# Two-layer decoder, attention of layers 0 and 1: SyncE issues a step's shift rows ahead of the loads of QK

## Chip, cores and metric

One core of one Trainium2 chip runs the whole program. The metric is the device time of one execution in microseconds (us), the median of several executions.

## What is computed

A decoder of two layers on x (32 batches, 128 tokens, width 128). Each layer is self attention, cross attention with a context, and a mixture of experts, each behind a layer norm and added to x:

```python
x = x + _L0_attn_ref(_layernorm(x), ...)            # 16 heads of width 8, 4 KV heads repeated
x = x + _L0_xattn_ref(_layernorm(x), ctx_1024, ...) # 16 heads of width 8
x = x + _L0_ffn_ref(_layernorm(x), ...)             # 8 experts, top 2, plus a shared one
x = x + _L1_attn_ref(_layernorm(x), ...)            # 4 averaged heads of width 64, relative bias
x = x + _L1_xattn_ref(_layernorm(x), ctx_1024, ctx_1024, mask, ...) # 16 heads of width 8, masked
x = x + _L1_ffn_ref(_layernorm(x), ...)             # 8 experts, top 2, plus a shared one
```

The three attentions with heads of width 8 go through the function `head_attention`: once for the two of layer 0 (tiles named `heads_...`, 64 batches in all), once for the cross attention of layer 1 (tiles named `cross_...`, 32 batches). For a batch and a head it is softmax(q k^T * scale) v.

## The kernel before, in words

`head_attention` is a software pipeline that each of the five instruction queues writes out by itself, step by step (`steps`, with one step per batch, a group being two batches). At step k:

- TensorE (`scores`) computes the scores of batch k+3 for their row maxima (`ps_max`, L973) and the transposed scores of batch k for the exponents (`ps_exp`, L977), in two parts v = 0 and 1; between them it turns the maxima of batch k+2 (L1045), and it projects q (even k) and k (odd k) of group k//2+5 (L1016, L1026).
- VectorE reduces the maxima (L776) and writes the shift of a batch as two bf16 numbers a head (L804). ScalarE copies the turned shift into `shiftT` (L870), takes the exponents (L847), and copies the projections out (L886, L890).
- GpSimd splits q and k of a group into three bf16 parts each (L690 to L693) and stores them to DRAM as `qk_parts` (L697, 384 KB a group).
- SyncE brings them back in the layout that the score products want: the tile `QK[p]` (four of them, one a group, used in turn) holds for each half of the heads 48 rows of parts and two rows for the shift. At an even step k it loads half 0 of group k//2+3, at the next step half 1 (L619, three DMAs of 192, 128 and 64 KB). At every step it places the two shift rows of batch k+2 (L629, two DMAs of 4 KB).

The shift rows of a batch go into the extra rows of the QK tile, so the exponent product of batch k yields scores minus maximum. It needs them when step k starts (`shift_placed`, waited for in `scores` at v = 0), two steps after they were issued. The first product of the maxima of group g is in step 2g-3 and needs both halves of the group's QK (`qk_placed`).

What SyncE waits for: before half 0, the store of that group (`qk_stored`, a semaphore that GpSimd's DMA raises) and the exponent scores of the batch before (`exp_scored`), since the tile is used again; before half 1, nothing of its own; before the shift rows, ScalarE's copy (`shiftT_ready`). SyncE works strictly in the order in which its program lists these, so whatever stands behind a wait waits too. In steps 22 to 50 of the `heads` part, and in the `cross` part, an even step also loads 128 KB of the context (`kvT`, L638), last in the step. All of SyncE's DMAs use one hardware queue.

The lines around the change are the function `emit` inside `sp_program`; who waits for them is in `scores`:

```python
if v == 0:
    pe.wait_ge(qk_placed[q_of], t.turn(96, 1, MA))
...
if v == 0:
    pe.wait_ge(shift_placed[t.k % 2], t.group(32, 32))
```

The loops that are rolled (`LOOPS`: steps 4 to 19 and 36 to 51 in the `heads` part, 4 to 11 in the `cross` part) use the same `emit`.

Of the kernel before, what the change touches and what calls it, by code (L numbers as in the profile page):

```python
# [24 lines left out]
B, S, D = 32, 128, 128  # L25
H, HD = 16, 8
G = 2
NG = B // G
GT = G * S
RING = 4  # L30
# [4 lines left out]
ROWS = sum(hi - lo for lo, hi in WINDOWS) * HD  # L35
HALVES = 2
HH = H // HALVES
BASE = 64
TILE, SLOT = 32, 16
SHIFT = 2  # L40
FA, SA, LA, MA, VA = 5, 4, 3, 3, 3
# [37 lines left out]
def need(engine, semaphore, value):  # L79

    if isinstance(value, int) and value <= 0:
        return
    engine.wait_ge(semaphore, value)


def apart(engine, t, turns):


    if t.reg is not None:
        engine.sem_inc(turns, 1)  # L90
# [313 lines left out]
def head_attention(nc, sem, name, x_sb, norm, ident, identb, QK, layers, mask, scale, prepare, opening, make_lead, staging, make_follow, handed):  # L404
# [14 lines left out]
    with ExitStack() as ctx:  # L419
        tiles = ExitStack()  # L420

        def sb(label, shape, dt=F32):
            return tiles.enter_context(nc.sbuf_tensor(f"{name}_{label}", shape, dt))
# [13 lines left out]
        NB_ALL, NG_ALL = NL * B, NL * NG  # L437
# [12 lines left out]
        shiftT = [sb(f"shiftT{p}", [SHIFT * H, S], BF16) for p in range(2)]  # L450
# [21 lines left out]
        turns_sp, turns_pool, turns_dve = sem("turns_sp"), sem("turns_pool"), sem("turns_dve")  # L472
# [23 lines left out]
        shiftT_ready = sem("shiftT_ready")  # L496
        shift_placed = [sem(f"shift_placed{p}") for p in range(2)]
# [39 lines left out]
        def slot(t, ahead=0):  # L537

            return (t.k // G + ahead) % RING

        def layer_of(t, group):

            return min((t.k // G + group) // NG, NL - 1)
# [29 lines left out]
        def load_qk_weights(engine, i):  # L573
            w = layers[i][0]
            for dst, src in ((wq, w["q"]), (wk, w["k"]), (bq, w["bq"]), (bk, w["bk"])):
                engine.dma_start(dst[i][:], src).then_inc(qk_loaded[i], 16)

        def load_vo_weights(engine, i):
            w = layers[i][0]
            for dst, src in ((wv, w["v"]), (wo, w["o"]), (bv, w["bv"]), (bo, w["bo"])):  # L580
                engine.dma_start(dst[i][:], src).then_inc(loaded[i], 16)

        def sp_program(sp):
            if kv_src[0] is not None:
                sp.dma_start(kvT[0][:], kv_src[0][:, 0:GT]).then_inc(kv_loaded[0], 16)
            if opening is not None:
                for i in range(len(Opening.PIECES) - 1):
                    opening.load_x(sp, i)
                opening.place_ones(sp, QK)
            for i in range(0 if opening is None else 1, NL):  # L590
                load_qk_weights(sp, i)
                load_vo_weights(sp, i)
            if opening is not None:
                opening.load_table(sp)
            if masked:
                sp.dma_start(mask_in[:, 0, :], mask[0]).then_inc(loaded[0], 16)
                for r in range(2):
                    sp.dma_start(mask_in[r * BASE:(r + 1) * BASE, 1, :], mask[1][(1 - r) * BASE:(2 - r) * BASE, :]).then_inc(loaded[0], 16)
            if lead is not None:
                prepare.load(sp, 0, 1, prepare.early(), prep_early)  # L600

            follow.sp_start(sp)

            def emit(t):
                if t.has(-2 * LA, 2 * NG_ALL - 1 - 2 * LA):

                    p, half = slot(t, LA), t.k % 2
                    if half == 0:
                        if opening is not None and t.k == -2 * LA:
                            sp.wait_ge(opening.ones_placed, 16 * HALVES * RING)  # L610
                        sp.wait_ge(qk_stored[p % 2], t.pair(16, LA, 1))
                        apart(sp, t, turns_sp)
                        need(sp, exp_scored, t.batch(PAIRS))
                        apart(sp, t, turns_sp)
                    row = 0
                    for lo, hi in WINDOWS:
                        n = (hi - lo) * HD
                        source = bass.AP(qk_dram[p], half * HH * GT, [[H * GT, n], [(PARTS + lo) * D * GT, 2], [1, HH * GT]])
                        sp.dma_start(QK[p][half * BASE + row:half * BASE + row + n].rearrange("r c h t -> r c (h t)"), source).then_inc(qk_placed[p], 16)  # L619
                        row += n  # L620
                if t.has(1 - MA, NB_ALL - MA):

                    p, j = (t.k + MA - 1) // G % RING, (t.k + MA - 1) % G
                    turned = shiftT[(t.k + MA - 1) % 2]
                    sp.wait_ge(shiftT_ready, t.batch(1, MA))
                    apart(sp, t, turns_sp)
                    for i in range(SHIFT):
                        at = ROWS + i
                        sp.dma_start(QK[p][at:at + BASE + 1:BASE, 0, :, j * S:j * S + S], turned[i:SHIFT * H:SHIFT, :]).then_inc(shift_placed[(t.k + MA - 1) % 2], 16)  # L629
                to = layer_of(t, FA + 1)  # L630
                if kv_src[to] is not None and t.k % 2 == 0 and t.has(-2 * FA, 2 * NG_ALL - 4 - 2 * FA):

                    p = slot(t, FA + 1)
                    need(sp, v_made, t.group(1, FA + 2 - RING))
                    apart(sp, t, turns_sp)
                    need(sp, qk_made, t.group(1, FA + 2 - RING))
                    apart(sp, t, turns_sp)
                    sp.dma_start(kvT[p][:], kv_src[to][:, bass.ds(t.group(GT, (FA + 1 - to * NG) * GT), GT)]).then_inc(kv_loaded[p], 16)  # L638
                if t.reg is None and prepare.splits and t.k in LATE_LOAD:
                    if t.k == LATE_LOAD[0]:  # L640
                        sp.wait_ge(prep_lo, Prepare.PIECES)
                    prepare.load(sp, LATE_LOAD.index(t.k), len(LATE_LOAD), prepare.late(), prep_late)
                if prepare.by_rel is not None and t.k == LAST:
                    prepare.load_bias(sp, by_rel_stored, bias_loaded)
                if t.reg is None and 0 <= t.k - CLEAR < CLEARS and follow.sp_clear is not None:
                    follow.sp_clear(sp, t.k - CLEAR)
                if t.reg is None and t.k == NB_ALL - 2 and follow.sp_tables is not None:
                    follow.sp_tables(sp)
            steps(sp, emit, FIRST, LOOPS, LAST)
            follow.sp(sp)  # L650

# [2142 lines left out]
```

## Time and profile before

| | |
|---|---|
| median of 3 executions | 1070.99 us (1059.96 to 1075.71) |
| the profiled execution | 1062.24 us, of it span 1060.1 us |
| granted TensorE clock, mean | 0.966 |
| PE / DVE / ACT / POOL busy | 917.9 / 823.2 / 664.8 / 648.1 us |
| `heads` part (scores on TensorE) | from 31 to about 355 us |
| `cross` part | from 726 to about 907 us |

PE is TensorE, DVE VectorE, ACT ScalarE, POOL GpSimd, SP SyncE; a q behind the name is the queue that issues (SPq, POOLq). In a row of the timeline the first number is the start in us, the second the duration; in brackets stands how long the engine was idle before and what ended it. A wait row reads: who waited, for whom, us in total, times, longest.

### The profile page before, as it was taken

To read this page: it belongs to the slowest core of one execution; us is meant where nothing else is said; L and a number is where in the kernel's file an instruction comes from. 1 tells how busy PE (TensorE), PEld (TensorE's weight loads), DVE (VectorE), ACT (ScalarE), POOL (GpSimd) and SP (SyncE) were. 2 spreads that over 40 slices of the span, in tenths; PEclk is the share of its full clock that TensorE was granted. 3 is DMA by queue.
4 is the path that set the end of the run, shared out by engine and by line. 5 is a ranking of instruction groups with operands and counts; after the bars stand their busy time and mean duration, and the time that the engine had idled before them with its cause. 6 is when DMAs were issued, how large, how long until landed. Compare 5 with 4: busy or idle time off the path is not lost.

```text
span 1060.1 us, 33068 instructions
## 1 busy us (share of the span) xinstructions
PE 917.9 (87%) x10494; PEld 673.0 (63%) x10494; DVE 823.2 (78%) x2110; ACT 664.8 (63%) x1609; POOL 648.1 (61%) x1020
## 2 busy tenths in 40 slices
PE   3599878889988789999998889977999998778997
PEld 1366656656665577777777677755566555556885
DVE  6389888878988778888897888766788766757675
ACT  1177777768776633555665888763666666556775
POOL 7857787887785467720585787158767842333443
PEclk9999999989998879999999999999999999889999
DMA  5776667886675201232332101125555650054551
GB/s 146 164 178 135 123 144 165 175 176 139 148 186 146 75 38 63 92 99 77 104 107 64 37 28 29 42 46 132 136 121 138 142 109 4 18 200 160 199 198 30
DMA packets 81455, 119.65 MB, mean 113 GB/s; under 512 B 16720, under 2 KB 62704, under 8 KB 80288
## 3 DMA queue, kind: packets, MB, share of 16 engines
q1 hardware_dynamic: 66704, 85.24, 32.6%
q0 software_dynamic: 9472, 27.27, 8.9%
q10 hardware_dynamic: 5136, 5.31, 2.3%
q8 instruction: 80, 1.31, 0.6%
q14 instruction: 63, 0.52, 0.2%
HBM read 80.75 MB, written 36.18 MB: 110 GB/s over the span
## 4 chain that ended last, share of the span: by engine, by line
PE 50%; DVE 19%; issue 9%; POOL 9%; DMA 7%; ACT 4%; SPq 1%; POOLq 1%; DVEq 0%; ACTq 0%
DVE heads_neg_max L776 4%; PE experts_ps_gu L2502 4%; PE cross_ps_max L963 3%; DVE cross_neg_max L776 3%; DMA QK<-heads_shiftT 3%; PE experts_ps_gu L2504 2%; PE experts_ps_gu L2503 2%; PE cross_ps_max L973 2%; DMA heads_qk_parts<-heads_parts 2%; PE cross_ps_pv L995 2%; PE heads_ps_max L973 2%; PE experts_ps_y L2523 2%; PE heads_ps_pv L995 2%; PE experts_ps_y L2524 2%; POOL heads_rest L691 2%
## 5 line engine op out<-in xcount | busy, mean ns | idle before, releaser
L776 DVE TENSOR_REDUCE heads_neg_max<-heads_ps_max 128x8 f32<-128x1024 f32 x128 | 156.4, 1222 | 50.2 <-PE heads_ps_max L973 48.3
L847 ACT ACTIVATE heads_E<-heads_ps_exp 128x1024 f32<-128x1024 f32 x128 | 131.1, 1024 | 71.5 <-PE heads_ps_exp L977 69.9
L973 PE MATMUL heads_ps_max<-QK 48*128 48x128 bf16 x1024 | 83.4, 227 | 37.5 <-DMA QK<-heads_shiftT 17.7
L776 DVE TENSOR_REDUCE cross_neg_max<-cross_ps_max 128x8 f32<-128x1024 f32 x64 | 78.4, 1225 | 36.7 <-PE cross_ps_max L973 36.5
L2196 POOL DMA_INDIRECT experts_gathered<-experts_y_dram,experts_index x64 | 62.1, 971 | 69.1 <-DMA experts_y_dram<-experts_y_sb 49.2
L973 PEld LDWEIGHTS heads_ps_max<-QK 48*128 48x128 bf16 x1024 | 60.6, 98 | 67.8 <-issue 29.3
L847 ACT ACTIVATE cross_E<-cross_ps_exp 128x1024 f32<-128x1024 f32 x64 | 65.6, 1025 | 57.3 <-PE cross_ps_exp L977 57.3
L2418 ACT ACTIVATE experts_act_out<-experts_ps_gu 128x256 f32<-128x256 f32 x110 | 42.4, 385 | 81.8 <-PE experts_ps_gu L2504 80.6
L995 PE MATMUL heads_ps_pv<-heads_E,heads_V 128*32 128x128 f32 x2048 | 85.9, 287 | 0.5 <-issue 0.5
L1627 POOL TENSOR_TENSOR experts_hidden_lo<-experts_hidden,experts_hidden_hi 128x512 fp32r<-128x512 f32 x32 | 41.4, 1295 | 70.6 <-ACT experts_hidden_hi L1851 67.3
L977 PE MATMUL heads_ps_exp<-QK 50*128 50x128 bf16 x1024 | 80.8, 223 | 0.7 <-ACT heads_E L847 0.6
L2172 POOL DMA_INDIRECT experts_xs_dram<-QK,experts_index x64 | 61.5, 962 | 28.0 <-DMA experts_xs_dram<-QK,experts_index 20.2
L2523 PE MATMUL experts_ps_y<-experts_down,experts_hT_hi 128*128 (+1 forms) x220 | 67.8, 329 | 6.6 <-DVE experts_hT_lo L2322 4.4
L995 PEld LDWEIGHTS heads_ps_pv<-heads_E,heads_V 128*32 128x32 f32 x2048 | 49.9, 112 | 28.2 <-issue 20.7
L2317 DVE TENSOR_TENSOR experts_hidden<-experts_act_out,experts_ps_gu 128x256 f32<-128x256 f32 x110 | 46.2, 420 | 25.7 <-ACT experts_act_out L2418 19.7
L1765 DVE TENSOR_TENSOR experts_hidden<-experts_ps_gate,experts_share 128x512 f32<-128x512 f32 x64 | 43.7, 688 | 24.0 <-ACT experts_ps_gate L1845 15.5
L977 PEld LDWEIGHTS heads_ps_exp<-QK 50*128 50x128 bf16 x1024 | 58.1, 97 | 1.5 <-ACT heads_E L847 1.0
L2524 PE MATMUL experts_ps_y<-experts_down,experts_hT_lo 128*128 (+1 forms) x220 | 58.1, 285 | 0.0
L1851 ACT CAST experts_hidden_hi<-experts_hidden 128x512 fp32r<-128x512 f32 x72 | 44.3, 615 | 20.8 <-DVE experts_hidden L1765 14.9
L1266 ACT ACTIVATE shared_E<-shared_scores,shared_neg_max 128x128 f32<-128x128 f32 x128 | 49.8, 393 | 6.7 <-DVE shared_probs L1215 6.7
L296 POOL TENSOR_TENSOR norm_var_eps<-norm_moments,norm_eps 128x2 f32<-128x2 f32 x64 | 12.6, 197 | 67.5 <-DVE norm_moments L289 57.1
L963 PE MATMUL cross_ps_max<-cross_drop_q,identb 64*64 64x512 bf16 x256 | 39.8, 387 | 10.2 <-DVE cross_neg_max L776 9.8
(323 smaller groups left out, 3134.3 us busy)
## 6 DMA issues: line engine op xcount, KB each, us to landing
experts_share<-experts_cT_dram SPq DMA_DIRECT2D x7, 2304.0 KB, 8.7
heads_qk_parts<-heads_parts POOLq DMA_DIRECT2D x32, 384.0 KB, 5.8
QK<-heads_qk_parts SPq DMA_DIRECT2D x64, 192.0 KB
QK<-heads_qk_parts SPq DMA_DIRECT2D x64, 128.0 KB
cross_qk_parts<-cross_parts POOLq DMA_DIRECT2D x16, 384.0 KB, 3.9
QK<-cross_qk_parts SPq DMA_DIRECT2D x32, 192.0 KB
experts_xs_dram<-load_stats SPq DMA_DIRECT2D x26, 192.0 KB, 2.8
experts_xs<-experts_xs_dram SPq DMA_DIRECT2D x78, 64.0 KB
```

Of the source, the lines that this page charges most:

```text
L776: nc.vector.tensor_reduce(neg_max[(t.k + MA) % 2][:, :, heads_of(v)], ps_max[:].rearrange("q a (h k) -> q a h k", h=HU), AX.X, ALU.max, ne ...
L847: nc.scalar.activation(E[:, :, heads_of(v), :], ps_exp[:].rearrange("k a (h q) -> k a h q", h=HU), ACT.Exp, scale=scale).then_inc(exp_done, 1)
L963: nc.tensor.matmul(ps_max[here, half, :].rearrange("q (h k) -> q h k", h=HU), identb[here, here], drop_q[here].unsqueeze(1).to_broadcast([ ...
L973: last_max = nc.tensor.matmul(ps_max[:, half, i * S:(i + 1) * S], QK[q_of][rows, 0, h, max_of], QK[q_of][rows, 1, h, max_of], start=not ma ...
L977: last_exp = nc.tensor.matmul(ps_exp[:, 1 - half, i * S:(i + 1) * S], QK[e_of][rows, 1, h, exp_of], QK[e_of][rows, 0, h, exp_of], start=no ...
L995: last = nc.tensor.matmul(ps_pv[TILE * i:TILE * (i + 1), v * S:(v + 1) * S], V[p][:, j, window:window + TILE], E[:, half, h, :], start=hal ...
L1266: last = nc.scalar.activation(E[:, s, :], scores[t.k % 2][:, s // 2, s % 2, :], ACT.Exp, bias=neg_max[t.k % 2][:, s:s + 1], accum_out=sums ...
L2172: pool.indirect_dma_start(xs_dram[h], bass.IndirectOffsetOnAxis(index[:, choice, b:b + 1], 0), xn[b // MG][:, b % MG, :], None).then_inc(s ...
L2196: pool.indirect_dma_start(gathered[n % GATHERS][:], None, y_dram[h], bass.IndirectOffsetOnAxis(index[:, choice, b:b + 1], 0)).then_inc(loa ...
L2317: nc.vector.tensor_tensor(hidden[u % 3][:], act_out[u % 3][:], ps_gu[:, u % 2, F:], ALU.mult).then_inc(hidden_ready, 1)
L2523: nc.tensor.matmul(out, hT_hi[u % 3][:, these], both, start=c == 0, stop=False, skip_group_check=True)
L2524: last = nc.tensor.matmul(out, hT_lo[u % 3][:, these], both, start=False, stop=c == 1, skip_group_check=True)
```

## The change

In `emit` of SyncE's program the block with the shift rows stands ahead of the block that loads QK, where it stood behind it. Waits, sizes, semaphores and the number of DMAs are the same.

```diff
             def emit(t):
+                if t.has(1 - MA, NB_ALL - MA):
+
+                    p, j = (t.k + MA - 1) // G % RING, (t.k + MA - 1) % G
+                    turned = shiftT[(t.k + MA - 1) % 2]
+                    sp.wait_ge(shiftT_ready, t.batch(1, MA))
+                    apart(sp, t, turns_sp)
+                    for i in range(SHIFT):
+                        at = ROWS + i
+                        sp.dma_start(QK[p][at:at + BASE + 1:BASE, 0, :, j * S:j * S + S], turned[i:SHIFT * H:SHIFT, :]).then_inc(shift_placed[(t.k + MA - 1) % 2], 16)
                 if t.has(-2 * LA, 2 * NG_ALL - 1 - 2 * LA):
...
-                if t.has(1 - MA, NB_ALL - MA):
-
...
```

Lines L605 to L613 are now the shift rows (their DMA is L613), and the loads' DMA is L628; before they were L629 and L619. The kernel's other lines keep their numbers.

SyncE's queue at the start of the `heads` part, before the change: the rows from half 0 of the third group on (`heads_qk_parts` are the stored parts, `heads_shiftT` the shift).

```order
L619 DMA QK<-heads_qk_parts 24x2x2048 [waits heads0_qk_stored0]
L619 DMA QK<-heads_qk_parts 16x2x2048
L619 DMA QK<-heads_qk_parts 8x2x2048
L629 DMA QK<-heads_shiftT 2x8x128 [waits heads0_shiftT_ready]
L629 DMA QK<-heads_shiftT 2x8x128
L619 DMA QK<-heads_qk_parts 24x2x2048
L619 DMA QK<-heads_qk_parts 16x2x2048
L619 DMA QK<-heads_qk_parts 8x2x2048
```

And after it, the same place:

```order
L613 DMA QK<-heads_shiftT 2x8x128 [waits heads0_shiftT_ready]
L613 DMA QK<-heads_shiftT 2x8x128
L628 DMA QK<-heads_qk_parts 24x2x2048 [waits heads0_qk_stored0]
L628 DMA QK<-heads_qk_parts 16x2x2048
L628 DMA QK<-heads_qk_parts 8x2x2048
L613 DMA QK<-heads_shiftT 2x8x128 [waits heads0_shiftT_ready]
L613 DMA QK<-heads_shiftT 2x8x128
L628 DMA QK<-heads_qk_parts 24x2x2048
```

The first batch's shift rows no longer stand behind the wait for the store of the third group, and half 1 of that group now stands behind the shift rows of the second batch.

In the rolled loop before the change, an even step and the odd step after it (QK1 is the group's tile, QK3 the one that gets the shift):

```order
L619 DMA QK1<-heads0_qk_parts1 24x2x2048 [waits heads0_exp_scored]
L619 DMA QK1<-heads0_qk_parts1 16x2x2048
L619 DMA QK1<-heads0_qk_parts1 8x2x2048
L625 ISA
L629 DMA QK3<-heads0_shiftT0 2x8x128 [waits heads0_shiftT_ready]
L629 DMA QK3<-heads0_shiftT0 2x8x128
L619 DMA QK1<-heads0_qk_parts1 24x2x2048
L619 DMA QK1<-heads0_qk_parts1 16x2x2048
L619 DMA QK1<-heads0_qk_parts1 8x2x2048
L625 REGISTER_ALU
L629 DMA QK3<-heads0_shiftT1 2x8x128 [waits heads0_shiftT_ready]
L629 DMA QK3<-heads0_shiftT1 2x8x128
```

After it:

```order
L613 DMA QK3<-heads0_shiftT0 2x8x128 [waits heads0_shiftT_ready]
L613 DMA QK3<-heads0_shiftT0 2x8x128
L620 ISA
L83 ISA [waits heads0_qk_stored1]
L628 DMA QK1<-heads0_qk_parts1 24x2x2048 [waits heads0_exp_scored]
L628 DMA QK1<-heads0_qk_parts1 16x2x2048
L628 DMA QK1<-heads0_qk_parts1 8x2x2048
L609 REGISTER_ALU
L613 DMA QK3<-heads0_shiftT1 2x8x128 [waits heads0_shiftT_ready]
L613 DMA QK3<-heads0_shiftT1 2x8x128
L628 DMA QK1<-heads0_qk_parts1 24x2x2048
L628 DMA QK1<-heads0_qk_parts1 16x2x2048
```

Half 1 stood right behind the even step's shift rows; now it stands behind the odd step's, which wait for ScalarE one step later. Half 0 stands behind the even step's.

## Rows read from the trace of the kernel before

**Rows 1.** The page, part 4: the chain that ended last, by line.

```profile
DVE heads_neg_max L776 4%; PE experts_ps_gu L2502 4%; PE cross_ps_max L963 3%; DVE cross_neg_max L776 3%; DMA QK<-heads_shiftT 3%; PE experts_ps_gu L2504 2%; PE experts_ps_gu L2503 2%; PE cross_ps_max L973 2%; DMA heads_qk_parts<-heads_parts 2%; PE cross_ps_pv L995 2%; PE heads_ps_max L973 2%; PE experts_ps_y L2523 2%; PE heads_ps_pv L995 2%; PE experts_ps_y L2524 2%; POOL heads_rest L691 2%
```

**Rows 2.** Waits of the whole span: us in total, times, longest.

```profile
PE heads_ps_max L973 <- DMA QK<-heads_shiftT: 17.7, 11, 6.3
...
PEld heads_ps_max L973 <- DMA QK<-heads_qk_parts: 5.1, 3, 2.8
```

**Rows 3.** Timeline of TensorE, first score products of steps -3, -1, 0.

```profile
30.85 0.35 PEld L973 LDWEIGHTS heads_ps_max<-QK 48*128 48x128 bf16 x8 [0.65 <-DMA QK<-heads_qk_parts]
...
41.92 0.62 PE L973 MATMUL heads_ps_max<-QK 48*128 48x128 bf16 x8 [2.11 <-DMA QK<-heads_qk_parts]
...
52.00 0.26 PE L973 MATMUL heads_ps_max<-QK 48*128 48x128 bf16 x1 [6.35 <-DMA QK<-heads_shiftT]
```

**Rows 4.** Timeline of SyncE's queue at the start of the heads part.

```profile
22.35 2.18 SPq L619 DMA_DIRECT2D QK<-heads_qk_parts  x6
...
45.18 1.32 SPq L629 DMA_DIRECT2D QK<-heads_shiftT  x2
...
47.82 1.07 SPq L629 DMA_DIRECT2D QK<-heads_shiftT  x2
```

**Rows 5.** Timeline of ScalarE: the copy of the first batch's shift.

```profile
37.49 0.26 ACT L870 COPY heads_shiftT<-heads_ps_qk 32x128 bf16<-32x128 bf16 x1 [0.18 <-PE heads_ps_qk L1045]
```

**Rows 6.** Timeline, first product of step 3 and of step 5 on TensorE.

```profile
66.27 0.23 PE L973 MATMUL heads_ps_max<-QK 48*128 48x128 bf16 x1
...
74.91 0.23 PE L973 MATMUL heads_ps_max<-QK 48*128 48x128 bf16 x1
```

**Rows 7.** SyncE's queue, half 1 of step 3, then shift rows of steps 3, 11.

```profile
65.68 1.42 SPq L619 DMA_DIRECT2D QK<-heads_qk_parts  x3
...
68.67 1.06 SPq L629 DMA_DIRECT2D QK<-heads_shiftT  x2
...
102.95 1.07 SPq L629 DMA_DIRECT2D QK<-heads_shiftT  x2
```

**Rows 8.** SyncE's queue: loads (L619), and the shift rows of steps 19, 25, 39, 53.

```profile
135.84 1.06 SPq L619 DMA_DIRECT2D QK<-heads_qk_parts  x3
...
139.71 1.16 SPq L629 DMA_DIRECT2D QK<-heads_shiftT  x2
...
171.44 1.06 SPq L629 DMA_DIRECT2D QK<-heads_shiftT  x2
...
208.84 1.26 SPq L619 DMA_DIRECT2D QK<-heads_qk_parts  x3
...
243.22 1.08 SPq L629 DMA_DIRECT2D QK<-heads_shiftT  x2
...
306.56 1.06 SPq L629 DMA_DIRECT2D QK<-heads_shiftT  x2
```

**Rows 9.** The chain in order of time: start us, us, the shift rows' transfer.

```profile
137.64 4.43 DMA QK<-heads_shiftT
...
211.83 6.59 DMA QK<-heads_shiftT
```

**Rows 10.** DMA issues in 78 to 97 us, 745 to 870 us: count, KB, us to landing.

```profile
heads_qk_parts<-heads_parts POOLq DMA_DIRECT2D x2, 384.0 KB, 4.8
...
cross_qk_parts<-cross_parts POOLq DMA_DIRECT2D x11, 384.0 KB, 3.6
```

**Rows 11.** Timeline of GpSimd: two stores of parts in a row.

```profile
110.61 0.91 POOL L697 DMA_DIRECT2D heads_qk_parts<-heads_parts  x1 [0.68 <-POOL heads_parts L693]
...
119.88 0.91 POOL L697 DMA_DIRECT2D heads_qk_parts<-heads_parts  x1 [0.75 <-POOL heads_parts L693]
```

**Rows 12.** Cross part: half 1 and shift rows of step 3, first product of step 5.

```profile
755.61 1.68 SPq L619 DMA_DIRECT2D QK<-cross_qk_parts  x3
...
759.25 1.06 SPq L629 DMA_DIRECT2D QK<-cross_shiftT  x2
...
767.27 0.23 PE L973 MATMUL cross_ps_max<-QK 48*128 48x128 bf16 x1
```

More of the change, by code:

```diff
@@ L620, in emit @@
                         row += n
-                if t.has(1 - MA, NB_ALL - MA):
[L623 to L629, printed above, removed]
                 to = layer_of(t, FA + 1)
```

## The prediction

> **What bounds the kernel now.** I read the page's chain first: it is spread thin, over TensorE, VectorE, GpSimd and DMA; what concerns this change is the 3% on the transfer of the shift rows and the 2% on the store of the parts [rows 1]. Outside the two stretches that run `head_attention` nothing is touched. The waits then say what stands against TensorE: 17.7 us for shift rows, 11 times, and 5.1 us for the parts [rows 2]. One of the 11 is 6.35 us before step 0; ahead of it, step -1 had waited 2.11 us for a load of QK [rows 3]. Why step 0 waited is seen on SyncE: ScalarE had the shift of batch 0 ready at 37.75 us [rows 5], its DMAs left only at 45.18 us [rows 4], since half 0 of the third group stood ahead and waited for GpSimd's store.
>
> The other ten (11.35 us) have the same shape in small. GpSimd stores a group every 9.27 us [rows 11]; the load of half 0 leaves when that store has landed, the shift rows behind it, and they travel behind its packets: issued at 137.09 us, after the load at 135.84, they land at 137.64 + 4.43 = 142.07 us [rows 8, 9]. They hold 8 KB, so nearly all of that is the load ahead of them.
>
> The pace is read from the issue times of the shift rows of odd steps, which follow TensorE's step by a fixed bit. A pair of steps (a group) took (102.95 - 68.67) / 4 = 8.57 us in steps 3 to 11, (139.71 - 102.95) / 4 = 9.19 in steps 11 to 19, (171.44 - 139.71) / 3 = 10.58 in 19 to 25, (243.22 - 171.44) / 7 = 10.25 in 25 to 39 (the stretch with the most other transfers), and (306.56 - 243.22) / 7 = 9.05 in 39 to 53 [rows 7, 8].
>
> **What is removed.** Shift rows no longer wait for a store or for half 0 of their own step. At the start they can leave at 37.8 us instead of 45.18, and step 0 can start about 4.2 us (half a pair) after step -1, at 46.1 instead of 52.00. Not all of the 5.9 us stays: step 1 needs group 2, whose half 0 still waits for the store that ends at about 44.1 us (half 0 left just ahead of the shift rows at 45.18) and whose half 1 follows at about 46.3. A pair of halves issued together was awaited for 30.85 - 22.35 = 8.5 us [rows 3, 4], so they are there at 52.6 to 55, and step 1, which began about 5.5 us after step 0, moves from 57.5 to 53 to 55. Bounds 0 and -5.9; I take -3 us.
>
> **What is added.** Both halves now leave later, and half 1 matters, for it is the last thing the next group needs. Take step 3: it starts at 66.27 us, half 1 left at 65.68, before the step even began; the shift rows of the step left at 68.67 [rows 6, 7]. After the change half 1 leaves behind them, 2.4 us (68.67 - 66.27) plus 1.1 us (two issues) into the step: at 69.8 us, 4.1 us later. Step 5, which needs it, started at 74.91 us. That leaves 5.1 us for a load that had 9.2. From then on the pair of steps can't be shorter than 2.4 + 1.1 + L = 3.5 + L, with L the time from issuing half 1 to its landing. The cover for the delay was the lead of the loads, and it is used up. Behind SyncE's new wait on ScalarE stand half 0, half 1 and the context loads; of these only half 1 has a reader within two steps (half 0 is issued a step earlier, and the context is read later).
>
> What is L? The trace gives the loads no landing, so it is bounded. From below by the nearest transfer of the same 384 KB, GpSimd's store, in 4.8 us in the heads part and 3.6 us in the cross part [rows 10]; the store reads 128 partitions where a load half writes 48, so I hold a load for hardly faster. From above by shift rows that travelled behind a load: load at 135.84, shift rows landed at 142.07, L at most 6.2 us in a quiet stretch; load at 208.84, shift rows landed at 211.83 + 6.59 = 218.42, at most 9.6 us in the dense one [rows 8, 9]. The pair in 8.5 us gives 4.3 us each as throughput, so one alone takes longer than that. I take 6.0 us in the quiet stretches, near the row of 6.2, and 8.0 us in the dense one, since the half before it will be a full step ahead instead of 2 to 3 us.
>
> A rule of the Trainium skill speaks for less: "DMA: Bandwidth & Descriptors", section "Anatomy of one DMA", fits a transfer by GpSimd's path as 2.0 us plus bytes / 436,000 per us, by which 393,216 bytes would need an estimated 2.9 us. By that rule L would fit into any pair and the loads' delay would cost nothing. The store, which is of just that kind, took 4.8 us here [rows 10], so the trace doesn't bear the fit out in this traffic; it counts for the rival with fast loads below.
>
> **The sum.** Quiet pair 3.5 + 6.0 = 9.5, dense pair 3.5 + 8.0 = 11.5:
> start -3; steps 3 to 11: 4 x (9.5 - 8.57) = +3.7; 11 to 19: 4 x (9.5 - 9.19) = +1.2; 19 to 25: 0 (L of 7 gives 10.5 against 10.58); 25 to 39: 7 x (11.5 - 10.25) = +8.8; 39 to 53: 7 x (9.5 - 9.05) = +3.2; two more pairs with loads after that, +1. Together +14.9, taken as +15 us. The 11.35 us of small waits for shift rows are inside these terms: they vanish, but the pair is then held by half 1, so they aren't subtracted again.
>
> In the cross part a pair takes 10.4 us, as TensorE itself is slower there. Half 1 would leave at 759.25 + 1.1 = 760.35 instead of 755.61, and is needed at 767.27: 6.9 us for a load, above the 6.2 [rows 12]. Term 0; TensorE's products hide it. If L were 8 there, it would cost 1.1 us in each of about 13 pairs.
>
> The profiled execution took 1062.24 us, so it would be 1077.2 us. The median of the three runs shown lies 8.75 us above the profiled one; I add half of that, about 4: 1081 us.
>
> **The rivals.**
> *Fast loads, faster.* If half 1 lands in 4.8 us, like the store, a quiet pair of 3.5 + 4.8 = 8.3 holds up nothing, and the waits for shift rows go. For it: the store's row, 17.7 us of waits removed. Against: the bound from the shift rows, and GpSimd's own 9.27 us a group, which would hold the middle stretches anyway. At its full 17.7 us: 1062.2 - 17.7 + 4 = 1049 us. It decides below an L of about 5.1 us.
> *GpSimd's pace hides it, no change.* With L at 5.6 a quiet pair is 9.1, about what it is now, as GpSimd stores every 9.27 us. Steps 3 to 11 cost 4 x 0.5 = +2, the start gives it back, and the dense pair with L at 6.7 is 10.2, as now. 1062.2 + 0 + 4 = 1066 us. For it: the middle stretches do look bound by GpSimd. Against: L must be well below both rows that bound it from above.
> *The dense stretch doesn't relax, much slower.* If L stays 9.6 us there, a pair is 13.1: 7 x 2.85 = +20 instead of +8.8; with 6.5 in the quiet pairs (+0.5 in 15 of them) the total is +34: 1062.2 + 34 + 4 = 1100 us. The cross part's +14 would belong to this case too. For it: the row of 9.6. Against: slower pairs thin the traffic out.
> That the change does not do what it says is excluded by the order of SyncE's queue.
>
> **How the numbers follow.** Forecast (+8 to +22) 0.40, no change (-5 to +8) 0.22, fast loads 0.12, much slower 0.26. Two per cent of the median is 21 us, about what a measurement can tell from no change. Faster by more: only the far end of fast loads, 0.03. Slower by more: 0.24 of the much slower case and 0.08 of the forecast, 0.32. The rest, 0.65, is within 2%. The range reaches down into fast loads, to 1054, and up past the much slower case to 1103; the forecast's own range is 1070 to 1092.
>
> **What would show it.** Right: the waits of TensorE for the shift rows fall from 17.7 us to under 3, and waits for `heads_qk_parts` rise from 5.1 to 20 us or more, all before odd steps; step 0 starts near 46 us; half 1 leaves 3.5 us into the odd step; pairs of 9.3 to 9.8 us in steps 3 to 19 and of 11 or more in 25 to 39; the cross part at 10.4 a pair with no wait for loads. Wrong: no waits for parts and pairs of 8.6 (L below 5.1), or GpSimd without a gap from step 5 to 20 and pairs of 9.2 with the waits elsewhere, or waits for parts in the cross part.

## The result, and the profile after

| | before | after |
|---|---|---|
| median (12 executions each) | 1060.56 us (1056.73 to 1075.71) | 1071.78 us (1068.27 to 1081.48) |
| ratio, 95% interval | | 1.0103 (1.0078 to 1.0128) |
| profiled execution, its span | 1062.24, 1060.1 us | 1070.25, 1068.2 us |
| granted TensorE clock, mean | 0.966 | 0.974 |

The change costs 1.0% (between 0.8 and 1.3%): slower, by less than the 2% that the forecast set as its mark. Between the medians it is 11.2 us, between the profiled executions 8.0: the one before lies 1.7 us above its median, the one after 1.5 below. The views below are of these two, so a few us of what they show can be theirs alone.

The chain that ended last, by line, in the page of after; it answers [rows 1]:

```profile
DMA QK<-heads_qk_parts 12%; PE experts_ps_gu L2502 4%; PE cross_ps_max L963 3%; DVE cross_neg_max L776 3%; SPq L613 3%; SPq L628 2%; PE experts_ps_gu L2504 2%; PE experts_ps_gu L2503 2%; PE cross_ps_max L973 2%; PE cross_ps_pv L995 2%; PE experts_ps_y L2523 2%; PE experts_ps_y L2524 2%; PE heads_ps_max L973 2%; PE experts_ps_hT L2510 2%; PE experts_ps_gate L1906 2%
```

The transfer of the shift rows (3% before) is gone from it, and the loads of QK, not among the lines listed before, head it with 12%, SyncE's issues (SPq) behind them. The waits say the same; they answer [rows 2]:

```profile
PE heads_ps_max L973 <- DMA QK<-heads_qk_parts: 36.2, 28, 4.6
POOL heads_parts L690 <- ACT heads_qk_full L890: 28.3, 19, 7.7
...
PEld heads_ps_max L973 <- DMA QK<-heads_qk_parts: 26.2, 15, 3.7
```

Waits for shift rows have left the list; those for the parts went from 7.2 us (5.1 of PEld [rows 2] and 2.1 of PE [rows 3]) to 62.4 us. PE and PEld are two views of TensorE that overlap, so this isn't 62 us of time. The middle row shows who waits in turn: GpSimd for ScalarE's copy of k (14.4 us before).

The timeline of TensorE, first score product of steps 0, 1, 3, 5, 7 and 17:

```profile
46.07 0.26 PE L973 MATMUL heads_ps_max<-QK 48*128 48x128 bf16 x1 [0.68 <-issue]
...
54.83 0.29 PE L973 MATMUL heads_ps_max<-QK 48*128 48x128 bf16 x1 [3.21 <-DMA QK<-heads_qk_parts]
...
65.31 0.23 PE L973 MATMUL heads_ps_max<-QK 48*128 48x128 bf16 x1
...
78.55 0.28 PE L973 MATMUL heads_ps_max<-QK 48*128 48x128 bf16 x1 [4.55 <-DMA QK<-heads_qk_parts]
...
89.57 0.23 PE L973 MATMUL heads_ps_max<-QK 48*128 48x128 bf16 x1
...
136.48 0.21 PE L973 MATMUL heads_ps_max<-QK 48*128 48x128 bf16 x1 [1.12 <-DMA QK<-heads_qk_parts]
```

SyncE's queue (now L613 the shift rows, L628 the loads): the start, then half 0 of step 2 (64.76), half 1 of steps 3, 15 and 31 (68.81, 130.49, 208.48), and the shift rows of steps 3, 11, 19, 25, 39 and 53:

```profile
37.30 1.12 SPq L613 DMA_DIRECT2D QK<-heads_shiftT  x2
...
45.99 1.20 SPq L628 DMA_DIRECT2D QK<-heads_qk_parts  x3
...
64.76 1.47 SPq L628 DMA_DIRECT2D QK<-heads_qk_parts  x3
67.70 1.06 SPq L613 DMA_DIRECT2D QK<-heads_shiftT  x2
68.81 1.46 SPq L628 DMA_DIRECT2D QK<-heads_qk_parts  x3
...
111.14 1.07 SPq L613 DMA_DIRECT2D QK<-heads_shiftT  x2
...
130.49 1.19 SPq L628 DMA_DIRECT2D QK<-heads_qk_parts  x3
...
148.18 1.07 SPq L613 DMA_DIRECT2D QK<-heads_shiftT  x2
...
176.64 1.07 SPq L613 DMA_DIRECT2D QK<-heads_shiftT  x2
...
208.48 1.28 SPq L628 DMA_DIRECT2D QK<-heads_qk_parts  x3
...
247.69 1.09 SPq L613 DMA_DIRECT2D QK<-heads_shiftT  x2
...
313.20 1.07 SPq L613 DMA_DIRECT2D QK<-heads_shiftT  x2
```

And the chain in order of time, which now gives the landing of half 1 (start plus duration; a row starts when the last of the three DMAs is issued):

```profile
46.87 7.92 DMA QK<-heads_qk_parts
...
69.94 8.29 DMA QK<-heads_qk_parts
...
131.36 4.89 DMA QK<-heads_qk_parts
...
209.44 6.54 DMA QK<-heads_qk_parts
```

Read them together: half 1 issued at 45.99 landed at 54.79, and step 1 began at 54.83; issued at 68.81 it landed at 78.23, step 5 began at 78.55; issued at 130.49 it landed at 136.25, step 17 began at 136.48. Step 3 began at 65.31 us, so its half 1 left 3.5 us into the step, and the pair up to step 5 took 13.2 us. Step 7 (89.57) had no wait for a transfer before it.

Where the 8 us came from, by the issue times of the shift rows of odd steps as for [rows 7, 8]:

| steps | a pair before | a pair after | change of the stretch |
|---|---|---|---|
| start, up to step 3 | | | 67.70 - 68.67 = -1.0 |
| 3 to 11 | 8.57 | 10.86 | +9.2 |
| 11 to 19 | 9.19 | 9.26 | +0.3 |
| 19 to 25 | 10.58 | 9.49 | -3.3 |
| 25 to 39 | 10.25 | 10.15 | -0.7 |
| 39 to 53 | 9.05 | 9.36 | +2.2 |
| sum at step 53 | | | 313.20 - 306.56 = +6.6 |

Issue times don't follow TensorE's step by a fixed bit everywhere: at step 25 before they came 3.75 us after its first product, at the table's other steps 2.4 to 2.7. By first products steps 19 to 25 and 25 to 39 change by -2.1 us each, instead of -3.3 and -0.7; their sum stays at -4. After step 53 the difference grows by 1.4 us more, 0.6 of it in the `cross` part.

The loss is not spread over the pairs. It is in steps 3 to 11 and, smaller, in 39 to 53; some comes back in 19 to 39, and the experiments show below that this last is not to be put down to the order. The waits of GpSimd tell 3 to 11 from 11 to 19, from 60 to 107 us and from 108 to 146 us:

```profile
POOL heads_parts L690 <- ACT heads_qk_full L890: 16.9, 3, 7.7
POOL heads_qk_parts L697 <- POOL heads_parts L693: 2.1, 4, 0.7
```

```profile
POOL heads_qk_parts L697 <- POOL heads_parts L693: 3.5, 5, 0.8
```

In the first stretch it stands 16.9 us for work from ScalarE, which follows a late TensorE. In the second it waits for nobody but the step before in its own queue: a pair takes the time that GpSimd needs for a group, before and after, and half 1's delay fits into that.

In steps 3 to 11 two things beside half 1's late start are seen. First, the issues of ScalarE's queue and of GpSimd beside the half 1 that took 9.4 us:

```profile
64.85 0.34 ACTq L223 DMA_DIRECT2D experts_whole<-in_experts_gate_up  x1
69.26 0.36 ACTq L223 DMA_DIRECT2D experts_whole<-in_experts_gate_up  x1
```

```profile
72.52 0.88 POOL L697 DMA_DIRECT2D heads_qk_parts<-heads_parts  x1 [0.29 <-POOL heads_parts L693]
```

A load of the experts' weights (256 to 320 KB) left 0.45 us behind half 1, and a store of parts while it travelled. Half 0 had left 4.05 us ahead of it (64.76). Second, the clock. Stretches of after (us, then busy time and count of each engine; the third number from the end is the granted clock):

```profile
69.00:74.00 5.00, 4.64 (x91) 3.15 (x90) 4.44 (x11) 4.33 (x10) 3.61 (x6) 1.00 0.96 146
74.00:78.00 4.00, 0.00 (x0) 0.00 (x0) 0.88 (x4) 0.01 (x1) 3.30 (x8) 0.99 0.83 204
78.00:86.00 8.00, 7.45 (x96) 5.54 (x100) 4.07 (x9) 3.55 (x7) 0.40 (x1) 0.58 0.29 70
```

TensorE did nothing for 4.55 us, and then ran at about half clock (1.2 GHz) for most of 8 us: 96 products in 8 us, 91 in 5 us ahead of it. The pair that began at 78.55 took 11.0 us (8.5 before), and since no transfer was awaited at its end, this isn't half 1's landing. No run changes the clock alone, so its share in these 2.5 us is argued from this row. In the kernel before the clock was whole here and fell in the dense stretch instead, in the same view of before:

```profile
168.00:171.00 3.00, 1.81 (x34) 1.25 (x28) 2.97 (x5) 1.61 (x4) 2.92 (x6) 1.00 1.07 265
171.00:176.00 5.00, 4.77 (x71) 3.29 (x71) 3.40 (x10) 2.47 (x7) 3.10 (x6) 0.66 0.72 117
```

The 0.66 over 5 us stand for 3.4 us at half clock. It did so four times between 171 and 237 us before, and never between 100 and 360 us after.

### The profile page after: what moved, and what is told of

Its sections match the earlier page's. It is cut to its first block, busy times and chain, and to the rows that moved or that the text cites. A ratio compares the mean times of both kernels' runs of the same rounds, so it can differ in the third digit from the quotient of the medians.

```text
span 1068.2 us, 33068 instructions
## 1 busy us (share of the span) xinstructions
PE 913.6 (86%) x10494; PEld 669.7 (63%) x10494; DVE 823.5 (77%) x2110; ACT 663.8 (62%) x1609; POOL 647.7 (61%) x1020
## 4 chain that ended last, share of the span: by engine, by line
PE 47%; DVE 15%; DMA 15%; issue 9%; SPq 5%; ACT 4%; POOL 4%; ACTq 0%; POOLq 0%; DVEq 0%
DMA QK<-heads_qk_parts 12%; PE experts_ps_gu L2502 4%; PE cross_ps_max L963 3%; DVE cross_neg_max L776 3%; SPq L613 3%; SPq L628 2%; PE experts_ps_gu L2504 2%; PE experts_ps_gu L2503 2%; PE cross_ps_max L973 2%; PE cross_ps_pv L995 2%; PE experts_ps_y L2523 2%; PE experts_ps_y L2524 2%; PE heads_ps_max L973 2%; PE experts_ps_hT L2510 2%; PE experts_ps_gate L1906 2%
## 5 line engine op out<-in xcount | busy, mean ns | idle before, releaser
L2196 POOL DMA_INDIRECT experts_gathered<-experts_y_dram,experts_index x64 | 62.3, 974 | 63.4 <-DMA experts_y_dram<-experts_y_sb 42.6
L2317 DVE TENSOR_TENSOR experts_hidden<-experts_act_out,experts_ps_gu 128x256 f32<-128x256 f32 x110 | 46.1, 419 | 25.0 <-ACT experts_act_out L2418 20.7
```

Source lines behind the costliest of these rows:

```text
L2196: pool.indirect_dma_start(gathered[n % GATHERS][:], None, y_dram[h], bass.IndirectOffsetOnAxis(index[:, choice, b:b + 1], 0)).then_inc(loa ...
L2317: nc.vector.tensor_tensor(hidden[u % 3][:], act_out[u % 3][:], ps_gu[:, u % 2, F:], ALU.mult).then_inc(hidden_ready, 1)
```

## Experiments

Each ratio is against the kernel before on the same chip in the same rounds, with its 95% interval. A version has 10 executions, e6 has 6, and e2, e4 and e11 have 4. The profiles are of one execution each. `place_shift` and `load_parts` stand for the two blocks of `emit`.

### One half of the change alone

`e1_even_first`: rows first at even steps only.

```diff
+                first, then = (place_shift, load_parts) if t.k % 2 == 0 else (load_parts, place_shift)
```

> Shift rows in front of the load at even steps only; at odd steps half 1 stays in front of them, so it leaves right behind half 0, about 4.6 us into the even step. Theory (the odd step is held by half 1, and the rows behind the store were the old loss): waits of TensorE for parts fall from 62 us (36.2 + 26.2) to under 10, waits for shift rows stay under 5, the middle stretches run at GpSimd's pace of 9.2 to 9.3 us a pair, steps 3 to 11 at about 8.6; ratio to before 0.985 to 0.995, so faster than both. Rival (the queue's traffic as a whole sets the pace, the order only moves the wait): pairs of 9.3 or more everywhere, ratio about 1.01 as with the whole change.

1067.48 against 1062.21 us, ratio 1.0045 (1.0013 to 1.0078). `e2_odd_first` has the other half (`if t.k % 2 == 1`).

> Shift rows in front of half 1 at odd steps only; at even steps half 0 stays in front of them as before. Theory: this is the part that costs; half 1 leaves 3.5 us into the odd step, waits for parts of 30 us or more, ratio 1.01 to 1.02, at least that of the whole change, as the start keeps its wait for the store. Rival (half 0's later place behind the even step's shift rows is what costs, since it pushes half 1 in the queue): ratio 1.00 to 1.005.

1077.38 us, ratio 1.0178 (1.0135 to 1.0221). The waits of e1, then of e2:

```profile
PE heads_ps_max L978 <- DMA QK<-heads_shiftT: 20.6, 15, 4.8
PEld heads_ps_max L978 <- DMA QK<-heads_qk_parts: 20.5, 11, 5.3
```

```profile
PE heads_ps_max L978 <- DMA QK<-heads_qk_parts: 29.5, 26, 2.4
...
PEld heads_ps_max L978 <- DMA QK<-heads_qk_parts: 20.7, 14, 3.1
...
PE heads_ps_max L978 <- DMA QK<-heads_shiftT: 7.2, 3, 5.7
```

The odd part, which puts half 1 behind ScalarE's copy of the odd step, carries the loss, as expected: alone it costs more than both parts together. The even part isn't free either, where a gain was expected (0.985 to 0.995, with under 5 us of waits for shift rows). Its waits show why: half 0 and half 1 now leave back to back, and the odd step's shift rows travel behind both. The next rows show it in e1, SyncE and TensorE:

```profile
65.85 1.89 SPq L620 DMA_DIRECT2D QK<-heads_qk_parts  x3
67.79 5.85 SPq L631 DMA_DIRECT2D QK<-heads_shiftT  x4
```

```profile
76.14 0.22 PE L978 MATMUL heads_ps_max<-QK 48*128 48x128 bf16 x1 [2.20 <-DMA QK<-heads_shiftT]
```

Step 5 needed the rows that step 3 issued at 67.79 us, and waited until 76.1 us for 8 KB. (The second row joins them with the rows of step 4.) By first products, steps 3 to 11 took 9.66 us a pair in e1, 9.54 in e2, 8.56 before and 10.79 after the whole change. e2 loses less there than the whole change and more later: steps 39 to 53 took 66.5 us, against 63.4 before and 65.6 after.

### The start alone

`e3_start_only`: the new order in the unrolled even steps with k < 0, the old one elsewhere.

```diff
+                first, then = (place_shift, load_parts) if t.reg is None and t.k < 0 and t.k % 2 == 0 else (load_parts, place_shift)
```

> The new order at step -2 alone (shift rows of batch 0 in front of half 0 of the third group), all other steps as before. Theory: step 0 starts near 46 us instead of 52, step 1 near 54.8 instead of 57.5, held by half 1 of the third group, and of that 2.7 us stays until GpSimd's stretch begins: ratio 0.997. Rival (the later waits for shift rows swallow the lead): ratio 1.000 and the same times from step 10 on.

1062.30 us, ratio 1.0010 (0.9996 to 1.0024): the rival, not the expected 0.997. Its step 1:

```profile
55.60 0.26 PE L978 MATMUL heads_ps_max<-QK 48*128 48x128 bf16 x1 [4.27 <-DMA QK<-heads_shiftT]
```

What step 0 had won, step 1 mostly waited for: the rows of the second batch, behind both halves. Step 0 began 6.2 us sooner than before (45.78), step 1 1.9, and step 3 at 66.41 no sooner (66.27 before).

This kernel has the old order from step 0 on, and is a yardstick for steps 19 to 39. By first products they took 103.7 us before and 99.5 after; here they took 99.8 us (137.68 to 237.49), and 99.7 in e9 below, both with the old order, but 103.6 in e5 (139.72 to 243.29), which has the new one. So the 4 us that "came back" differ from execution to execution and are not shown to be a gain of the order. They are also about what the difference of the medians (11.2) has more than that of the profiled executions (8.0).

### Neither behind the other: the rows on ScalarE's queue

`e4_shift_on_act`: the block leaves SyncE; ScalarE issues the two DMAs right after its copy.

```diff
+                    act.wait_ge(shiftT_ready, t.batch(1, MA))
...
+                        act.dma_start(QK[p][at:at + BASE + 1:BASE, 0, :, j * S:j * S + S], shiftT[q][i:SHIFT * H:SHIFT, :]).then_inc(shift_placed[q], 16)
```

> ScalarE issues the shift rows itself behind its copy, on its own DMA queue; SyncE only loads. Theory: neither wait exists any more, loads leave as soon as the store has landed, waits for shift rows and parts together under 10 us; ratio 0.985 to 0.995 as with the even-only order, if the two issues (1.1 us a step on ScalarE, which is busy 63%) hide. Rival (ScalarE has no room: the exponents of part 1 come 1.1 us later in each step): pairs of 9.5 or more, ratio 1.00 to 1.02.

1099.41 us, ratio 1.0373 (1.0319 to 1.0427). Its ScalarE, one step, and its heaviest wait in the `heads` part:

```profile
94.97 0.25 ACT L861 COPY heads_shiftT<-heads_ps_qk 32x128 bf16<-32x128 bf16 x1
95.25 1.07 ACTq L866 DMA_DIRECT2D QK<-heads_shiftT  x2
96.51 0.37 ACT L874 COPY heads_xnT<-heads_ps_xv 128x256 f32<-128x256 f32 x1 [1.29 <-issue]
```

```profile
DVE heads_neg_max L767 <- PE heads_ps_max L969: 78.9, 81, 11.7
```

And a wait of TensorE that had been small:

```profile
PE heads_ps_qk L1012 <- ACT heads_xnT L874: 25.6, 31, 1.4
```

Both waits of TensorE for SyncE's transfers are small (5.0 us for rows, 12.9 for parts), and it is the slowest kernel of the study, beyond the theory and its rival. ScalarE stands 1.29 us in the issues ahead of its next work. In even steps that is the copy `heads_xnT`, for which TensorE's projection waited 31 times, 25.6 us in all (2.0 us before). The pairs of the `heads` part are now 10.0 to 10.5 us everywhere. So the steps lose where a pair had been shorter: 6.4, 3.8 and 7.4 us in steps 3 to 11, 11 to 19 and 39 to 53, and nothing in 19 to 39. The `cross` part loses 9.6 us (11.1 us a pair, 10.4 before).

### Other transfers beside half 1

`e5_weights_early`: the changed kernel, with the loads of the experts' weights that ScalarE's queue spreads over steps -4 to 3 moved to steps -10 to -3. `e9_weights_early_old`: the same with the old order.

```diff
-        WORK, BULK = LOOPS[0][1], (-4, 4)
+        WORK, BULK = LOOPS[0][1], (-10, -2)
```

> The new order, with ScalarE's eight loads of expert weights in steps -10 to -3 instead of -4 to 3. Theory: the long landing of half 1 in steps 3 to 6 (69.9 to 78.2 us, 9.4 us from its issue) comes from these loads running beside it, so pairs of steps 3 to 11 fall from 10.8 to about 9.4 us and the ratio to before from 1.010 to 1.005; a later step -3 (31 us now) may take part of it back. Rival (GpSimd's store beside it is what lengthens it, or the loads cost as much wherever they stand): pairs of 10 or more there, ratio 1.01.

> The old order with ScalarE's loads of expert weights in steps -10 to -3: the yardstick for the same move in the new order. Theory (their place only matters to the new order, where half 1 has no time left): ratio 0.999 to 1.002, steps 3 to 11 at 8.6 us a pair as before, so the new order's loss with early weights is 0.5% against 1.0% with late ones. Rival (the loads are in the way of both orders): ratio about 0.995, and the new order's loss stays 1.0%.

e5: 1066.47 against 1062.73 us, ratio 1.0050 (1.0025 to 1.0076). e9: 1060.68 against 1063.43 us, 0.9984 (0.9954 to 1.0013). So with these loads out of the way the new order costs about 0.7% (1.0050 / 0.9984) where it cost 1.0%: some 4 us of the loss is their company, and the three intervals together allow anything from nothing to about twice that. The profiled executions say it more clearly for steps 3 to 11. In the same stretch, e5 and then e9:

```profile
55.00:100.00 45.00, 39.08 (x692) 27.92 (x685) 36.02 (x77) 31.37 (x63) 27.90 (x52) 1.00 0.52 114
```

```profile
55.00:100.00 45.00, 42.44 (x798) 30.48 (x791) 39.37 (x87) 35.04 (x71) 31.87 (x58) 1.00 0.58 135
```

The clock no longer falls here with the new order, and the pairs of steps 3 to 11 (first products of TensorE) come to 9.64 us, against 8.59 in e9: with the company gone, the plain delay of half 1 costs 4 x 1.05 = 4.2 us there.

The weights' load alone doesn't make 9.4 us, though. In e2 it stands just as close behind half 1 of step 3, which was issued at 70.50 us, and GpSimd's store follows at 73.98:

```profile
70.73 0.33 ACTq L223 DMA_DIRECT2D experts_whole<-in_experts_gate_up  x1
```

```profile
71.37 5.47 DMA QK<-heads_qk_parts
```

That half 1 landed at 76.84, after 6.3 us. What differs most is half 0: in e2 it had left 8.9 us ahead, in the changed kernel 4.05. With half 0 as close but the weights gone (e5: 63.92 and 67.97) half 1 took 6.9 us. So the 9.4 us came where both were close to it. That is read from one execution of each kernel; no run moves half 0 alone.

`e10_even_first_weights_early` joins this with e1.

> Shift rows in front at even steps only, and the weights early. Theory (what the even-only order lost was in steps 1 to 9, where the odd step's rows travelled behind two halves and the weights): steps 3 to 11 from 9.66 to about 8.9 us a pair, ratio to before 0.998 to 1.001; no gain beyond, since GpSimd's 9.2 us a group holds the rest. Rival (the rows behind two halves cost everywhere): ratio 1.004.

1064.86 us, ratio 1.0013 (0.9981 to 1.0045): not told from before, and not better than e9. Steps 3 to 11 took 9.11 us a pair, between e1's 9.66 and the 8.9 expected.

### Half 1 small

`e6_small_half1_new` and `e7_small_half1_old` load, from the fifth group on, only an eighth of the columns of half 1, with the new and with the old order; the scores of seven of the sixteen heads are then computed from what the tile held before, so their results are wrong and only their times count.

```diff
+                        cols = HH * GT if half == 0 or (t.reg is None and t.k < 2) else GT
```

> The new order; from the fifth group on half 1 loads only one head's columns of eight (48 rows as before, 1/8 of the bytes), so the rest of the half keeps what was loaded before: the products run on old data. Theory (half 1's landing sets each odd step): waits for parts fall from 62 us to under 10, pairs at GpSimd's 9.2 or less, time at or under that of the same reduction in the old order. Rival (the late place in the queue costs by itself, or half 0 does): still 0.5% or more above the old order with the same reduction.

> The old order with the same reduction of half 1 as in the run before (one head's columns of eight from the fifth group on). It is the yardstick for that run. Theory: shift rows travel behind half 0 only, so some of their waits stay where SyncE waits for the store; ratio to before 0.985 to 0.995. Rival (GpSimd's pace is all there is): ratio 0.997 to 1.00.

1049.87 us, ratio 0.9901 (0.9871 to 0.9930), and 1052.53 us, 0.9923 (0.9888 to 0.9958). The waits for the parts in e6:

```profile
PEld heads_ps_max L974 <- DMA QK<-heads_qk_parts: 8.4, 5, 3.6
...
PE heads_ps_max L974 <- DMA QK<-heads_qk_parts: 5.7, 3, 2.9
```

When half 1 is short the order costs nothing that shows (1.0% with the full one), though SyncE issues as late in the step as in the changed kernel. The profiled executions agree stretch by stretch: steps 3 to 11, 11 to 19, 19 to 39 and 39 to 53 took 34.3, 36.0, 94.0 and 63.9 us with the new order, 34.4, 35.8, 93.9 and 63.8 with the old. So the loss needs a full half 1. The smaller load also thins the traffic for everything else (both kernels are 0.8 to 1.0% faster than before), so these two alone can't tell its own landing from what it does to others; e2, and the landings just ahead of the steps, say that it is the landing. TensorE's waits for parts in e6, 14.1 us, are above the 10 expected; 13.0 of them lie at the start, ahead of the smaller loads.

In steps 11 to 19 the pair stays at 9.0 us in both kernels (before 9.15, by first products), with seven eighths of half 1's bytes gone. GpSimd's stores are 9.2 to 9.3 us apart there in both, as before [rows 11]: its group holds the pace, whatever the loads do.

### Half 1 sooner, with the rows still first

`e8_half1_split`: the first DMA of half 1 (192 of 384 KB) is issued at the even step behind half 0, the other two in the odd step behind the shift rows.

```diff
-                    row = 0
-                    for lo, hi in WINDOWS:
...
+                    for which, pieces in ((half, WINDOWS[half:]),) + (((1, WINDOWS[:1]),) if half == 0 else ()):
```

> The new order, but the first DMA of half 1 (24 rows, 192 of its 384 KB) leaves in the even step behind half 0; the other two stay behind the odd step's shift rows. Theory: what is left of half 1 lands in about 4.5 us instead of 5.5 to 6, so it holds a quiet pair to 8.0, below GpSimd's 9.2, and the odd step's shift rows, now behind one and a half loads, land 4.5 us after their issue, with 6.5 us to spare: waits for parts and rows together under 25 us, ratio to before 0.99 to 1.00. Rival (the packets of both halves and the store fill the queue whatever their order, so a wait comes back at the rows): ratio 1.003 to 1.008, like the even-only order.

1066.86 us, ratio 1.0050 (1.0020 to 1.0080), half of the loss back, where all of it was expected. The ratio is the rival's, but not its mechanism: no wait for the rows is listed, and those for parts are still 38.1 us. Steps 3 to 11 took 10.03 us a pair.

`e11_half1_at_wait`: at odd steps SyncE waits for ScalarE, then issues half 1, then the rows. It takes away the 1.1 us of two issues from half 1's delay and leaves the 2.4 us of the wait.

```diff
+                if t.k % 2 == 1 and t.has(1 - MA, NB_ALL - MA):
...
+                    load_parts()
+                    place_shift()
```

> As the new order, but at odd steps half 1 leaves after the same wait for ScalarE and in front of the two shift rows' issues: 1.1 us earlier, and the rows 1.1 us later. Theory (a pair is 2.4 + 1.1 + L, all of it on the path): where half 1 holds the step a pair gets up to 1.1 us shorter, until GpSimd's 9.2 holds: steps 3 to 11 from 10.8 to 9.8, the stretches at 9.4 to 9.2; ratio to before 1.003 to 1.006. Rival (the wait for ScalarE alone counts, or the rows behind a full half 1 then hold the next odd step): ratio 1.010 or more, with waits for rows above 10 us.

1075.35 us, ratio 1.0117 (1.0059 to 1.0175): not better than the change, as the rival had it, though the interval of four executions is wide. Its waits, and its step 5:

```profile
PE heads_ps_max L983 <- DMA QK<-heads_shiftT: 28.9, 18, 5.2
...
PEld heads_ps_max L983 <- DMA QK<-heads_qk_parts: 26.2, 13, 5.6
```

```profile
78.61 0.22 PE L983 MATMUL heads_ps_max<-QK 48*128 48x128 bf16 x1 [2.62 <-DMA QK<-heads_shiftT]
```

The parts are still awaited 26.2 us, and the rows, now behind a load that itself left late, 28.9 us. Step 5 stands where it stood in the changed kernel (78.55), with the rows as what comes last. This is the trade in one row: on one queue, what is moved ahead takes its time from what is moved behind, and here both have a reader at the same product. The theory's pairs did get shorter, 10.06 us in steps 3 to 11 and 8.84 in 11 to 19 (10.79 and 9.31 after the change), and at step 53 this kernel was 2.1 us ahead of the changed one. Steps 53 to 60 then took 35.0 us against 30.6, and it was behind; why is open.

## Why the prediction was right, and where it wasn't

The forecast was 1081 us, within 2% of before. The direction and the mechanism held, and the sum was too high: +15 us, where the profiled executions differ by 8.0 and the medians by 11.2. By its own steps:

- **The start, -3 us with step 0 at 46.1 and step 1 at 53 to 55.** Step 0 began at 46.07, step 1 at 54.83, held by half 1 of the third group, as said. Of the 2.7 us won at step 1, 1.0 were left by step 3. And e3 shows that the lead alone is worth nothing that can be told (0.9996 to 1.0024).
- **Half 1 leaves 3.5 us into the odd step, and the pair is 3.5 + L.** Both hold (65.31, 68.81), and step 17 starts 0.23 us after the landing. e6 against e7, with e2, confirm that this is where the cost is.
- **L of 6.0 us in quiet stretches.** Right: 136.25 - 130.49 = 5.8, the bounds 4.8 to 6.2 hold. (The 4.8 was of two stores; the page of before has 5.8 as the median of all 32 in the `heads` part.) The estimate by the Trainium skill's rule, 2.9 us for this size ("DMA: Bandwidth & Descriptors", "Anatomy of one DMA"), was half of what the trace shows. The Trainium skill gives that fit per DMA on GpSimd's path; these loads are SyncE's, three DMAs each, with other transfers beside them.
- **Steps 3 to 11, +3.7 us.** Mis-sized: +9.2. I called this stretch quiet, and it has the last weights' loads, a store and a close half 0 beside half 1. L was 9.4 in its first pair, the row of 9.6 that I had put down for the dense stretch alone [rows 8, 9]. The first pair alone took 13.2 us instead of 8.6. The 4.55 us without a product were followed by the half clock, which wasn't in the working at all, and by a pair of 11.0. With the weights moved (e5 against e9) the term is 4.2, so its arithmetic was sound for the traffic that it assumed.
- **Steps 11 to 19, +1.2 and 39 to 53, +3.2.** Measured +0.3 and +2.2. L was 5.4 to 5.9 us in the quiet pairs whose landing the chain shows, so 3.5 + L was 8.9 to 9.4, at GpSimd's pace and not above it.
- **Steps 19 to 25, 0, and 25 to 39, +8.8 us.** Measured -3.3 and -0.7 (-2.1 each by first products): the term that was mis-sized most. L of 8.0 was wrong. At the same place as the bound of 9.6, half 1 now landed at 209.44 + 6.54 = 215.98, issued at 208.48: 7.5 us, and if all these pairs were held by it the mean L was 10.15 - 3.5 = 6.65. The row of 9.6 was a bound by the shift rows issued 3 us behind a load, and I took a value close to it. So a pair was what it had been, not 1.25 us longer. That it came out shorter isn't the order's doing as far as the runs show: e3 and e9, with the old order, have the same time for steps 19 to 39 as the changed kernel, and e5, with the new one, that of before. The clock was down four times for 3.4 us here before and not after, but e5 was as slow as before with two falls and e3 as fast as after with two, so it doesn't settle this.
- **The cross part, 0.** Right. TensorE's start there is shifted by 6.1 us, and it is shifted by 6.1 at its step 20 too; then 0.6 us are lost before step 21. TensorE's weight loads waited twice for parts there, 1.3 us in all, where none was forecast. The slack of 0.7 us (6.9 against 6.2) was just about enough.
- **+4 us for the median.** Of no use: over 12 executions the kernel before has its median 1.7 us below its profiled execution, not 8.75 above. The median of three had two high ones.

Of the rivals, "GpSimd's pace hides it" is what happened in steps 11 to 19: +0.3 us there, with GpSimd waiting for nobody. It is also a part of why the 11.35 us of small waits for shift rows brought so little when they went: three of the ten, 2.1 us, lay in that stretch and only passed time that GpSimd's next group needed. Most of the others lay between 142 and 219 us, where new waits for half 1 took their place. In 3 to 11, where a pair had been shorter than its group (8.57 against 9.27), there was no such cover.

Of what was to show it right, the waits, step 0 and the place of half 1 are seen in the rows above. The pairs are not: 10.8 in steps 3 to 11 and 10.15 in 25 to 39, where 9.3 to 9.8 and 11 or more were named. And two of the signs of being wrong came in part: GpSimd without a gap, in steps 11 to 19, and a small wait for parts in the `cross` part. Two errors in the sum had opposite signs (+5.5 in steps 3 to 11, -12.8 in 19 to 39), so that the total looks closer than its terms. That they offset each other is luck.

What stays open: how the 9.4 us of half 1 in step 3 are shared between the weights' load, half 0 and GpSimd's store, which no run moved; what the half clock alone costs; and what sets the 4 us by which executions differ in steps 19 to 39. No version with right results was found that beats the kernel before beyond its interval; e9 is the nearest, with 0.9984 (0.9954 to 1.0013).

## What to carry to other kernels

On a shared queue a small urgent transfer can't be moved ahead for nothing: if it waits for something, all that stands behind it inherits the wait. Look for the reader of the last item behind it and count its slack (here 5.1 us for a load of 5.8). Removing a wait gives back only time that no other engine needs anyway. Bound a transfer's time from the stretch in which it will travel, with the other queues' issues of that stretch at hand, not from the name of the stretch. And compare a stretch over several kernels that agree in it before a gain there is credited to the change.

## What the runs showed of the hardware

- A pause of TensorE can cost more than its length: after 4.55 us with no product it ran its products at half clock for most of 8 us (granted 0.58 over 78 to 86 us), and the pair took 11.0 us, the two after it 9.8 and 9.2. A fall also came without such a pause, in the kernel before between 171 and 176 us, with 34 products from 168 to 171 us. The distance of two score products is 0.10 to 0.11 us then (78.63, 78.73, 78.84) and 0.05 to 0.06 else (65.38, 65.44, 65.49); the Trainium skill, "TensorE: Matmul & The Clock Gate", section "Wait — 56ns, not 53.3ns?", has 106.7 and 55.6 ns for products of this width at 1.2 and 2.4 GHz, and the trace agrees.
- The record of the clock isn't complete. From 54.83 us on the products also stood 0.11 us apart (54.91, 55.02, 55.13), while the granted clock of that stretch is given as 1.00; the first record of the clock in this trace is at 60.9 us. The Trainium skill warns on the same page, "TensorE: Matmul & The Clock Gate", in "Seeing it yourself", that such events were seen to be unreliable.
- Two issues of 4 KB DMAs took the issuing engine 1.05 to 1.3 us, on SyncE and on ScalarE. On SyncE they delay only what stands behind them (1.1 of half 1's 3.5 us); the kernel with them on ScalarE was 37 us slower (e4).
- The same 384 KB load took from 5.1 us (issued at 149.29, landed at 154.43) to 9.4 us (68.81) from its first issue, by what travelled with it.
